# The fifth order's product with the values, on VectorE at the fourth expert instead of GpSimd

## The reference

```
Tv = Tk * v[:, :, :, None, :]                 # each order's key polynomial times the values
kv_prefix = jnp.cumsum(Tv, axis=2)            # prefix sum over the tokens
kv_beta = kv_prefix * beta[None, None, None, :, None]
num = (Tq * kv_beta).sum(axis=3)              # sum over the orders
den = (Tq.sum(axis=-1) * k_beta).sum(axis=3)
out_h = num / (den[..., None] + EPS_DEN)
```

## Time and profile before

| | us |
|---|---|
| median of 3 runs | 990.74 (985.78, 991.19, 990.74) |
| the profiled execution's own time | 988.04 |
| its span, first to last instruction | 986.3 |
| PE busy | 863.2 |
| DVE busy | 832.3 |
| ACT busy | 440.8 |
| POOL busy | 461.1 |

### The profile page before, as it was taken

One profiled execution on the slowest core, in us unless ns is written; L12 is line 12 of the kernel. 1 busy time (PEld: TensorE's weight loads), 2 busy tenths in 40 slices (PEclk: granted clock), 3 DMA queues, 4 the chain that ended last, 5 costly groups with the idle time before them and its releaser, 6 DMA issues. The chain is left out here.

```text
span 986.3 us, 14280 instructions
## 1 busy us (share of the span) xinstructions
PE 863.2 (88%) x4377; PEld 641.4 (65%) x4377; DVE 832.3 (84%) x1319; ACT 440.8 (45%) x637; POOL 461.1 (47%) x631
## 2 busy tenths in 40 slices
PE   3862658999898999999999999899999999978995
PEld 3641426676666767676767676686767676747784
DVE  2478798999899999999999999999999999987421
ACT  4253425363545545353635455554535363431420
POOL 2013445273546547472747365554837175453210
PEclk9777778999999999999999999999999999999998
DMA  7104133344452546353543536353634243443431
GB/s 256 49 1 87 43 68 127 75 102 128 74 160 66 151 88 161 65 142 77 117 120 72 149 69 176 68 150 80 167 65 125 69 103 113 79 128 75 126 108 21
DMA packets 51948, 101.03 MB, mean 102 GB/s; under 512 B 5347, under 2 KB 34606, under 8 KB 49846
## 3 DMA queue, kind: packets, MB, share of 16 engines
q1 hardware_dynamic: 35106, 65.45, 20.4%
q0 software_dynamic: 15360, 33.56, 19.9%
q10 hardware_dynamic: 1428, 1.43, 0.5%
HBM read 57.68 MB, written 17.58 MB: 76 GB/s over the span
## 5 line engine op out<-in xcount | busy, mean ns | idle before, releaser
L1383 PE MATMUL acc<-w,hid 128*128 128x256 f32 x1152 | 272.6, 382 | 14.6 <-DVE hid L1110 14.6
L1383 PEld LDWEIGHTS acc<-w,hid 128*128 128x128 f32 x1152 | 215.1, 190 | 58.9 <-DVE hid L1110 27.0
L813 ACT ACTIVATE hid<-ring,b1row 128x512 f32<-128x512 f32 x144 | 98.5, 684 | 180.3 <-PE ring L1264 179.0
L657 POOL DMA_DIRECT2D feat<-feat x48 | 46.5, 968 | 273.8 <-DVE feat L987 132.3
L1110 DVE TENSOR_TENSOR hid<-hid,cfw 128x512 f32<-128x512 f32 x128 | 92.9, 728 | 43.6 <-DMA cfw<-cf_rows 28.1
L768 ACT ACTIVATE feat<-ring,bqkv 128x512 f32<-128x512 f32 x96 | 66.1, 689 | 116.6 <-PE ring L1264 116.6
L1341 PE MATMUL tr<-wo_g,feat 128*128 128x256 f32 x256 | 67.1, 421 | 47.1 <-DVE feat L1029 47.1
L1264 PE MATMUL ring<-n2H,w1H 128*128 128x512 f32 x288 | 102.5, 437 | 0.0
L962 DVE TENSOR_TENSOR_SCAN feat<-zero,carry,feat 128x512 f32<-128x512 f32 x80 | 99.2, 1289 | 0.0
L962 DVE TENSOR_TENSOR_SCAN feat<-zero,feat 128x512 f32<-128x512 f32 x80 | 94.5, 1230 | 0.0
L1341 PEld LDWEIGHTS tr<-wo_g,feat 128*128 128x128 f32 x256 | 52.7, 211 | 61.0 <-DVE feat L1029 45.0
(11 more groups left out here) (152 smaller groups left out, 1550.8 us busy)
## 6 DMA issues: line engine op xcount, KB each, us to landing
feat<-feat POOLq DMA_DIRECT2D x48, 512.0 KB, 4.6
cfw<-cf_rows SPq DMA_DIRECT2D x16, 1280.0 KB, 7.7
xin<-in_L_attn_x SPq DMA_DIRECT2D x16, 512.0 KB, 9.5
feat<-inv_rows SPq DMA_DIRECT2D x32, 256.0 KB
out<-x SPq DMA_DIRECT2D x16, 512.0 KB, 8.6
cfw<-cf_rows SPq DMA_DIRECT2D x16, 512.0 KB, 3.6
out<-fin POOLq DMA_DIRECT2D x16, 512.0 KB, 6.1
cfw<-cf_rows SPq DMA_DIRECT2D x16, 256.0 KB, 4.7
```

The costliest lines, as they stand in the source:

```text
L657: g.dma_start(f(into), f(of), accum_op=ALU.add).then_inc(added[n], 16)
L813: a.activation(hid[:, e % NG], ring[bank][:, :], ACT.Silu, bias=b1row[:, e:e + 1]).then_inc(ring_copied, 1)
L1383: last = mm(acc[t // 2][:, t % 2], hid[:, e % NG, t * P:(t + 1) * P], w2[:, e], start=False, stop=(e == E), skip_group_check=True)
```

## The change

`weigh_order_5` and its semaphore go. VectorE computes the fifth order's product with the same operands (KT5 times V0 into W+4) directly behind `expert(3)`, ahead of the product of order 2. All five products count on `weighted`, and the waits of ScalarE and of the prefix sums are rewritten to this count.

```diff
-            def weigh_order_5(i, p):
-
-                c = number(i, p)
-                pool.wait_ge(odd_ready, 4 * c + 2)
-                ge(pool, numerator, c)
-                g.tensor_tensor(f(W + 4), f(KT5), f(V0), ALU.mult).then_inc(weighted5, 1)
-
...
                 if st["attn"]:
-                    weigh_order_5(i, p)
                     if p == 0:
                         scale_wo(i)
...
                 if m >= 4:
-                    ge(act, weighted, (ND - 1) * number(i, p))
-                    ge(act, weighted5, number(i, p))
+                    ge(act, weighted, ND * number(i, p))
...
-            BY_WEIGHT = (0, 1, 3, 2)
+            BY_WEIGHT = (0, 1, 3, 4, 2)
...
-                    dve.wait_ge(odd_ready, 4 * c + 1)
-                    v.tensor_tensor(f(W + n), f(KT3), val, ALU.mult).then_inc(weighted, 1)
+                    dve.wait_ge(odd_ready, 4 * c + n // 2)
+                    v.tensor_tensor(f(W + n), f(KT3 if n == 2 else KT5), val, ALU.mult).then_inc(weighted, 1)
...
-                if n < 4:
-                    dve.wait_ge(weighted, (ND - 1) * c + BY_WEIGHT.index(n) + 1)
-                else:
-                    dve.wait_ge(weighted5, c + 1)
+                dve.wait_ge(weighted, ND * c + BY_WEIGHT.index(n) + 1)
...
                 expert(3)
                 if attn_:
                     weigh(i, p, 3)
+                    weigh(i, p, 4)
                     prefix(i, p, 2)
                     prefix(i, p, 3)
                 expert(4)
```

More of the change, by code:

```diff
@@ L230, in build @@
         weighted = sem("values_weighted")
-        weighted5 = sem("values_weighted_order_5")
         scanned = sem("prefix_sums")
@@ L780, in square @@
                     if q == 0:
-                        ge(act, weighted, (ND - 1) * c)
-                        ge(act, weighted5, c)
+                        ge(act, weighted, ND * c)
                     else:
```

## The result

The changed kernel took 1004.81 us in the median (1000.27 to 1007.75, 4 runs), the kernel before 989.84 (985.78 to 991.19, 4 runs): ratio 1.0147, 95% interval 1.0105 to 1.019. In a second comparison, on one chip with three experiments, it was 1.0198 (1.0176 to 1.022). So it is slower by 15 to 20 us. I had forecast 12.5 us for the profiled execution and 1002 us in all.

What follows compares the result with a forecast made beforehand. Bound by a loop: DVE from n2L to divide, then PE from the output projection to n2L. 18.1 - 2.6 - 2.5 - 0.5 = +12.5 us gave 1000.5 or 1003.2, taken as 1002; forecast range 996 to 1009, 8-in-10 range 992 to 1011.

Steps and rivals of the forecast that it cites:

- Two stretches that take turns: A 53.5 us middle step: DVE sets 30.2 us from n2L to divide, PE sets 23.3 us from there to n2L.
- 1.13 us per product: Behind expert(3), in DVE's stretch: each of 16 added products delays the queue 1.13 us, 18.1 us in all.
- late scalings: Three p = 0 steps: scale_wo, delayed by GpSimd's product, slowed L987 behind n2L; without it 2.5 us come back.
- GpSimd's hold worth little: Of 25.6 us in which GpSimd's product held DVE, mostly between divide and n2L, only the exceptions come back: 2.6, 2.5, 0.5 us.
- 2.6 - 1.1 = 1.4 forecast: Step 0: L925 and L927 lose their delays, 2.6 us come back; one added product costs 1.13 us.
- The step that had taken 23.77 us: One step, divide to n2L: a held prefix sum outlasted n2H, 23.77 us against 23.30 elsewhere; 0.5 us come back.
- The rival in which all 25.6 us count: DVE sets the whole step, so all its held time counts: -11 us, 977 us; chance 8%.
- Transfer of the inverse covers the product: In front of divide: DVE's 10.9 us of waits for the spread inverse swallow most of the product, +1.6 us, 990; chance 12%.
- The clock, kept as a rival of 10%: Output projection to n2L: granted clock falls in half of 12 other steps, 10 us more, 1012 us; chance 10%.
- already counted in the period: PE's second matmuls of experts 5 to 8: PE idles about 1 us more per step, with no separate cost.
- PE's busy time: Whole run: PE's busy time stays as it was.

Runs made afterwards that it cites:

- e1_slack: Changed kernel with the fifth order's product moved from behind expert(3) to directly ahead of lows(1), where VectorE waits for n2H; ratio 0.9979 to the kernel before.
- e6_two_in_slack: Changed kernel with both the fifth order's and the order 2 product moved ahead of lows(1), where VectorE waits for n2H; 972.65 us, ratio 0.9853 to the kernel before.
- e2_no_product: Kernel before without GpSimd's product; ScalarE copies KT5 into W+4 instead, leaving the values out of this order; ratio 0.9958 to the kernel before.
- e4_changed: The changed kernel again, unaltered, as reference beside other experiments on one chip; ratio 1.0198 to the kernel before.
- e3_twice: Kernel before, GpSimd's product kept, with VectorE's order 2 product computed twice, ahead of and behind expert(3); ratio 1.0247 to the kernel before.
- e5_hold: Changed kernel plus one GpSimd multiplication of 128 x 400 per attention step, inside VectorE's stretch from n2L to divide; ratio 1.028 to the kernel before.
- e7_fill: Changed kernel plus four extra TensorE matmuls of 512 columns ahead of the output projection; 998.96 us, ratio 1.0127 to the kernel before.

## Why the prediction was right, and where it was off

- **Two stretches that take turns.** Right, and shown by e1_slack: the same operation costs 1.2 us per step in one stretch (355.6 - 338.0 us over 15 steps of n2L to issue) and next to nothing in the other, where the wait for n2H shrank by 16.5 of the 18.1 us. e6_two_in_slack moved a second one across and gained 12 us more between the medians' ratios (0.9979 to 0.9853), where 13 were expected.
- **1.13 us per product.** Right. n2L to issue grew by 14.5 us over 15 steps; the forecast was 15 x 1.13 - 2.5 = 14.5. Step by step it is 0.9 to 1.4 us, but 0.74, 0.21 and 0.07 in the three steps that had the late scalings: there the relief of 0.42, 0.95 and 1.10 us comes off.
- **GpSimd's hold worth little.** Right: 4.2 us in e2_no_product, for 5.6. In step 0 the two operations that had taken 2.70 and 2.29 us take 1.22 each:

```profile
57.76 1.22 DVE L914 SCALAR_TENSOR_TENSOR feat<-feat 128x1024 f32<-128x1024 f32 x1 [0.81 <-ACT feat L777]
58.90 1.22 DVE L916 SCALAR_TENSOR_TENSOR feat<-feat 128x1024 f32<-128x1024 f32 x1
```

The first `divide` came 1.3 us earlier, for 2.6 - 1.1 = 1.4 forecast, but that match is luck in part: over all profiles it stands between 92.45 and 96.80 us, and VectorE did wait 0.51 us at 79.99 in the kernel before, where the prediction saw no wait. No late L987 of 1.6 to 2.3 us was left (1.48 is the longest now). In e4_changed there is one of 2.01 us at 617.93 with no product of GpSimd to make it: `expert(2)`, and with it the gate's rows, came late there through the wait for the weights' transfer. The step that had taken 23.77 us from `divide` to n2L takes 23.28. The rival in which all 25.6 us count (977 us) fell with e1_slack and e2_no_product.
- **Transfer of the inverse covers the product.** Wrong as a rival, as I had argued: the wait for it didn't shrink but was 14.2 us instead of 10.9.
- **What was off: two terms at nothing.** The sum gave 12.5 us, and the comparisons gave 15 and 19.6 us for the change and 24.4 for the doubled product, for 18.1. The first comparison's interval, 10 to 19 us, holds 12.5; e4_changed's, 17 to 22, doesn't. In the span of e4_changed's profiled execution, 21.5 us longer than before, the forecast parts came out as forecast within 1 us (n2L to issue 14.7). The surplus of 9 us is 5.5 us between the issue of the inverse and `divide`, and 3.4 between `divide` and n2L (2.9 more than before, where the sum had 0.5 less). The sum had nothing for either.
- **The clock, kept as a rival of 10%, is a term.** The sentence that doesn't hold is that TensorE's added idle time was "already counted in the period". With the product in VectorE's stretch the clock fell in 1, 3, 4 and 0 of the 12 full steps (first profile, e4_changed, e3_twice, e5_hold); without it in 1, 0, 0 and 1 (before, e1_slack, e2_no_product, e6_two_in_slack). Each fall costs 1.6 to 1.8 us. I had put 10 us on this rival with the right mechanism, as one or the other, where it was some of it in some executions. How much of the price it is in the median stays open between the 2 and the 7 us of e7_fill.
- **A late inverse comes first.** Every fall in a full step stood where the issue to `divide` took 7.8 us or more, against 7.0 to 7.3 us as a rule. e5_hold has the longest stretch of VectorE and no such step, and no fall. So the product alone doesn't make the clock fall; a slow transfer costs its own delay and, most times, a fall on top.
- **The first profiled execution's own surplus** (17.7 us of span for 12.5) was mostly that transfer: 3.9 us from the issue of the inverse to `divide`. Over all the profiles this part is between 109.6 and 115.7 us, and e5_hold and e7_fill, with the product in the same place as the changed kernel, have 110.6 and 109.6. So it varies between executions, and these profiles don't show it as a price of the change. What makes a transfer slow in one of them stays open.
- **Also off:** PE's busy time was forecast unchanged and is 871.1 us instead of 863.2. No run here prices that difference.

## What to carry to other kernels

When two engines are both near 90% busy, find the points in the period at which one waits for the other, and cut it there; each stretch has one engine that sets it, and an operation is worth its length or nothing according to the stretch it stands in. Before an operation goes to another engine, look whether that engine has a wait a few instructions away: moving the product by a few lines was worth 2% here, more than the choice between VectorE and GpSimd. And an engine that waits longer may come back slower: where a transfer can come late ahead of TensorE's work, its spread between executions and the clock behind it belong into the range of the sum.

## What the runs showed of the hardware

From step 2 on, all falls of the clock at the output projection stood behind a gap of 1.88 us or more there (1.88, 2.99 and 2.58 in the full steps of e4_changed), and none behind a shorter one. Step 14, which isn't among the full ones, had one in e4_changed (2.71 us) and e5_hold (2.84 us) too. But a long gap isn't enough. The first row is of e1_slack, the second of e6_two_in_slack:

```profile
368.20 3.72 PE L1328 MATMUL tr<-wo_g,feat 128*128 128x256 f32 x16 [3.20 <-DVE feat L1015]
```
```profile
362.84 5.41 PE L1328 MATMUL tr<-wo_g,feat 128*128 128x256 f32 x16 [2.70 <-DVE feat L1015]
```

After 3.20 us without a matmul the clock held, and after 2.70 it fell. Idle time of TensorE shortly before doesn't decide it either: in the 10 us ahead of the gap TensorE was busy for 9.26 us in e1_slack, where the clock held, and for all 10.00 in e6_two_in_slack, where it fell. What decides stays open.

An operation of GpSimd that nobody waits for isn't free, and not lost either: the same hold of VectorE was worth little in one stretch (e2_no_product: 4.2 us of the 29 held) and 0.70 us per operation in the other (e5_hold).
